# First stage of a graph network: range pairs, edge counts and tile loads in another order, and a buffer of its own for tile 9

## The reference

```
x1  = layernorm(x)
xl  = x1 @ W1;  res = x1 @ Wr1                        # layer 1: 4 heads of 256, "dense" and "res1"
e   = leaky_relu(alpha_src[src] + alpha_dst[dst])      # alpha = sums of xl * a_src1, xl * a_dst1
h   = relu(layernorm(segment_softmax(e) weighted sum of xl[src] + b1)) + res + br1
h   = the same with one head of 768 (W2, Wr2)          # layer 2
x   = x + h
g   = softmax(layernorm(x) @ Fr + fbr);  top 2 of 8 experts per node
out = x + sum over the two experts of g * (gelu(layernorm(x) @ F1[e] + fb1[e]) @ F2[e] + fb2[e])
```

## Time and profile before

| | us |
|---|---|
| median of 3 runs | 1108.69 |
| the runs | 1107.84, 1112.44, 1108.69 |
| the profiled execution, its own time | 1107.56 |
| its span in the trace | 1105.8 |

### The profile page before, as it was taken

The page is one execution under the profiler, slowest core; times in us unless marked ns, Lnnn a source line. Parts: engine busy times, 40 slices in busy tenths (PEclk is TensorE's granted clock), DMA queues, the critical chain, the costliest instruction groups (busy, mean ns, idle before and its releaser), DMA issues.

```text
span 1105.8 us, 15213 instructions
## 1 busy us (share of the span) xinstructions
PE 1048.9 (95%) x4364; PEld 696.6 (63%) x4365; DVE 700.1 (63%) x1708; ACT 357.4 (32%) x632; POOL 140.1 (13%) x266
## 2 busy tenths in 40 slices
PE   5999999999999999999999999999999779999993
PEld 3467777755588888855556556556666546665661
DVE  5998899579677777879466517866777533223222
ACT  0222321233477777611001014820001223333331
POOL 3000010000000000011000000102222213324332
PEclk9999999999999999999999999999999899999997
DMA  9535556611134001072121100332448755484432
GB/s 265 190 115 208 206 202 215 225 44 52 44 117 184 21 1 38 1 200 80 58 75 48 46 29 29 93 147 86 118 117 311 243 196 183 146 306 126 152 108 91
DMA packets 53567, 141.44 MB, mean 128 GB/s; under 512 B 8346, under 2 KB 17082, under 8 KB 53250
## 3 DMA queue, kind: packets, MB, share of 16 engines
q1 hardware_dynamic: 42321, 109.17, 29.4%
q0 software_dynamic: 8160, 23.16, 6.6%
q10 hardware_dynamic: 3024, 8.36, 2.7%
HBM read 81.89 MB, written 61.48 MB: 130 GB/s over the span
## 4 chain that ended last, share of the span: by engine, by line
issue 38%; PE 36%; DMA 11%; DVE 10%; DVEq 2%; POOL 1%; SPq 1%; POOLq 0%; ACT 0%
PE PSA L1887 9%; PE PSA L1828 8%; PE PSA L1817 7%; DMA RX<-out,RX 6%; PE PSA L1947 3%; PE PSA L1961 3%; DVE RW2X L880 2%; DMA out<-RX 2%; DVE RB L894 1%; DVE RX L1244 1%; DVE RW2X L882 1%; DVEq L803 1%; PE PSA L1908 1%; DMA xs_d<-RB,RW2X 1%; DMA RB<-xr_d 1%
## 5 line engine op out<-in xcount | busy, mean ns | idle before, releaser
L1801 PE MATMUL PSA<-RW2X 125*125 125x257 f32 x800 | 173.9, 380 | 0.0
L1801 PEld LDWEIGHTS PSA<-RW2X 125*125 125x125 f32 x800 | 149.8, 188 | 24.4 <-DVE RW2X L962 0.8
L1887 PE MATMUL PSA<-RW2X,RW 125*125 125x385 f32 (+1 forms) x360 | 122.0, 489 | 0.0
L1620 PE MATMUL PSA<-RW,RX 128*125 128x512 f32 x240 | 109.9, 607 | 1.9 <-ACT RX L1319 1.9
L1828 PE MATMUL PSA<-RW2X,RX 128*125 128x384 f32 x320 | 107.3, 488 | 1.9 <-DVE RW2X L1040 1.9
L1638 PE MATMUL PSA<-RW,RX 128*125 128x512 f32 (+2 forms) x360 | 107.4, 452 | 0.0
L1817 PE MATMUL PSA<-RW2X,RX 128*125 128x384 f32 x320 | 105.1, 487 | 2.2 <-ACT RX L1439 1.4
L1428 ACT ACTIVATE RW2X<-RX,RK 125x625 f32<-125x625 f32 x120 | 91.5, 811 | 31.3 <-PE PSA L1801 31.3
L1961 PE MATMUL PSA<-RW2X 128*128 x276 | 96.4, 500 | 2.7 <-issue 1.0
L956 DVE TENSOR_TENSOR RW2X<-RW2X 125x625 f32<-125x625 f32 x80 | 64.8, 810 | 53.7 <-ACT RW2X L1428 53.6
L1947 PE MATMUL PSA<-RW2X,RX 128*128 x276 | 96.4, 499 | 1.9 <-ACT RX L1522 1.1
(11 more groups left out here) (337 smaller groups left out, 1273.0 us busy)
## 6 DMA issues: line engine op xcount, KB each, us to landing
xs_d<-RB SPq DMA_DIRECT2D x10, 3108.0 KB, 11.2
RW2X<-in_L_ffn_W SPq DMA_DIRECT2D x16, 1152.0 KB, 8.3
RW2X<-xs_d ACTq DMA_DIRECT2D x21, 388.5 KB
RX<-res_d SPq DMA_DIRECT2D x10, 448.0 KB
RX<-in_x SPq DMA_DIRECT2D x12, 336.0 KB
RX<-adm_d SPq DMA_DIRECT2D x6, 610.4 KB
xr_d<-RW2X SPq DMA_DIRECT2D x10, 336.0 KB
res_d<-RB SPq DMA_DIRECT2D x7, 448.0 KB
```

What stands on the lines that cost most here:

```text
L1620: last = mm(ps[res_bank(n)][0:TP, :], xTt[t][:, kk, :], wr1s[:, kk, j * 512:(j + 1) * 512], start=(kk == 0), stop=(kk == KD - 1))
L1801: last = mm(ps[n % 7][0:TP, 0:XW], ering[:, (p * NT + m) % EBUF, 0, i * TP:(i + 1) * TP], xl[:, m, p // 2, :], start=(m == 0), stop=(m == ...
L1887: last = mm(ps[PAIR[t % 3][c]][0:TP, 0:DW - c], p2[m][:, t * TP:(t + 1) * TP], xl2[:, m, c, 0:DW - c], start=(m == 0), stop=(m == NT - 1))
```

## The change

In the first stage:

- DVE: the normalisation of tile 0 comes ahead of the conversion of the edge lists; the norm of tile 1 ahead of the wait for PE's edge transposes, instead of behind the table; the 48 sums behind pair 2 and the norm of tile 4, instead of ahead of them.
- PE: half of res1(0) comes ahead of the edge transposes, turn_x(1) and 4 of 6 products of res1(1) ahead of the rows of the ranges. Between the dense products the hists move: hist(2) behind dense(0, 0) and dense(0, 1), dense(1, 0) ahead of dense(0, 2), and turn_x goes from tile t + 4 to t + 3. Tile 0 has one hist fewer, tile 9 two more (`WIN`).
- ACT: its copies follow PE's order; `nth` gives the place of a dense part in the new order.
- SP: the first half of `Wr1` is loaded in two parts with semaphores of their own, and tiles 2 and 3 have their own load ahead of tiles 4 to 9.

In the last layer, tile 9 has a third buffer `xr[2]`, at the start of RX where `ya` (the sum of an expert's output) lies later. Its load stands behind the store of tile 1 and waits for no other store; and `drain(0)`, the first to write `ya`, waits for the store of tile 9.

```diff
-WIN = (2, 2, 2, 2, 2, 2, 3, 3, 3, 2)
+WIN = (1, 2, 2, 2, 2, 2, 2, 3, 3, 4)
...
         ya = f(D)
+        xr.append(ya[0:TP, :])
...
+        def xb(t):
+            return 2 if t == NT - 1 else t % 2
...
-            for j in range(2):
-                sp.dma_start(wr1s[:, :, j * 512:(j + 1) * 512],
...
+            sp.dma_start(wr1s[:, 0:KD // 2, 0:512], wr1_in[:, 0:KD // 2, 0:512]).then_inc(ld_wr1_top, 16)
+            sp.dma_start(wr1s[:, KD // 2:KD, 0:512], wr1_in[:, KD // 2:KD, 0:512]).then_inc(ld_wr1[0], 16)
+            rows(sp, xall[:, 1, :], x_t[1], ld_x1)
+            sp.dma_start(wr1s[:, :, 512:C1], wr1_in[:, :, 512:C1]).then_inc(ld_wr1[1], 16)
+            rows(sp, xall[:, 2:4, :], x_t[2:4].rearrange("t p d -> p t d"), ld_x23)
+            rows(sp, xall[:, 4:NT, :], x_t[4:NT].rearrange("t p d -> p t d"), ld_x)
...
-                rows(sp, out_t[t], xr[t % 2], x1_stored[t % 2])
-                if t + 2 < NT:
+                rows(sp, out_t[t], xr[xb(t)], x1_stored[xb(t)])
+                if t == 1:
+                    load_xr(NT - 1)
+                if t + 2 < NT - 1:
...
             norm_stats(0)
+            norm_apply(0)
             dve.wait_ge(ld_e, 32)
...
-            norm_apply(0)
...
+            dve.wait_ge(ld_x1, 32)
+            norm_stats(1)
 
             dve.wait_ge(edges_turned, 1)
...
             v.tensor_copy(tab_i, tab_f[:, 3, :]).then_inc(table_ready, 1)
-            dve.wait_ge(ld_x1, 32)
-            norm_stats(1)
...
-                if p == 1:
+                if p == 2:
                     wa1_sums()
...
-                if not (isinstance(n, int) and n == 0):
+                if isinstance(n, int) and n == 0:
+                    dve.wait_ge(x1_stored[2], 32)
+                else:
                     dve.wait_ge(y_ready, n)
...
             turn_x(0)
+            pe.wait_ge(xt_ready, 2)
+            pe.wait_ge(ld_wr1_top, 16)
+            res1(0, 0, KD // 2)
             pe.wait_ge(edges_ready, 1)
...
-            pe.wait_ge(xt_ready, 2)
-            res1(0)
+            pe.wait_ge(ld_wr1[0], 16)
+            res1(0, KD // 2, KD)
+            turn_x(1)
+            res1(1, 0, 4)
             pe.wait_ge(range_cols, 1)
...
-            res1(1)
+            res1(1, 4, KD)
...
-                res1(2 * t + 1)
-                turn_x(t + 1)
-            w = 2
-            for t in range(NT):
+                if t == 1:
+                    res1(2 * t + 1, 0, KD // 2)
+                    turn_x(t + 1)
+                    res1(2 * t + 1, KD // 2, KD)
+                else:
+                    turn_x(t + 1)
+                    res1(2 * t + 1)
+            dense(0, 0)
+            dense(0, 1)
+            hist(2)
+            dense(1, 0)
+            dense(0, 2)
+            turn_x(4)
+            hist(3)
+            dense(1, 1)
+            dense(1, 2)
+            hist(4)
+            w = 5
+            for t in range(2, NT):
                 pe.wait_ge(xt_ready, 2 * t + 2)
                 dense(t, 0)
+                if t + 3 < NT:
+                    turn_x(t + 3)
                 hist(w)
                 dense(t, 1)
+                if t >= 7:
+                    hist(w + 1)
                 dense(t, 2)
-                if t + 4 < NT:
-                    turn_x(t + 4)
-                for i in range(1, WIN[t]):
+                for i in range(2 if t >= 7 else 1, WIN[t]):
                     hist(w + i)
```

More of the change, by code:

```diff
@@ L333, in gnn_ffn @@
         ld_x1 = sem("ld_x1")
+        ld_x23 = sem("ld_x23")
         ld_x = sem("ld_x")
@@ L421, in gnn_ffn @@
         norm2_done = sem("norm2_done")
-        xr_loaded = [sem(f"xr_loaded{i}") for i in range(2)]
+        xr_loaded = [sem(f"xr_loaded{i}") for i in range(3)]
         x1_ready = sem("x1_ready")
-        x1_stored = [sem(f"x1_stored{i}") for i in range(2)]
+        x1_stored = [sem(f"x1_stored{i}") for i in range(3)]
         xf_ready = sem("xf_ready")
@@ L461, in gnn_ffn, with nth @@
         block = ctx.enter_context(nc.Block())
+        def nth(t, c):
+            return {(1, 0): 2, (0, 2): 3}.get((t, c), 3 * t + c)
         def res_bank(n):
@@ L489, in _ @@
             sp.dma_start(e_i[:, 1, :], dst.rearrange("(g e) -> g e", g=EG)).then_inc(ld_e, 16)
[L490 to L495 removed]
+            wr1_in = Wr1.rearrange("(k p) c -> p k c", p=128)
+            sp.dma_start(wr1s[:, 0:KD // 2, 0:512], wr1_in[:, 0:KD // 2, 0:512]).then_inc(ld_wr1_top, 16)
[4 more added lines that the diff above has]
+            rows(sp, xall[:, 4:NT, :], x_t[4:NT].rearrange("t p d -> p t d"), ld_x)
             sp.dma_start(abc[:, 0, :], a_src1.rearrange("h c -> (h c)")[None, :].to_broadcast([128, C1])).then_inc(ld_a, 16)
@@ L586, in load_xr @@
             def load_xr(t):
-                rows(sp, xr[t % 2], xr_d[t], xr_loaded[t % 2])
+                rows(sp, xr[xb(t)], xr_d[t], xr_loaded[xb(t)])
             for i in range(2):
@@ L642, in _ @@
                 sp.sem_inc(w_ready, 1)
-            for i in range(2):
-                sp.wait_ge(x1_stored[i], 32 * HT)
+            for i in range(3):
+                sp.wait_ge(x1_stored[i], 32 * (HT, HT - 1, 1)[i])
         @block.gpsimd
@@ L770, in _ @@
             pool.wait_ge(slots_ready, 1)
-            for i in range(2):
-                pool.wait_ge(x1_stored[i], 32 * HT)
+            for i in range(3):
+                pool.wait_ge(x1_stored[i], 32 * (HT, HT - 1, 1)[i])
             total = pool.value_load(slot_i[0:1, 2, 7:8], min_val=EARLY + 1, max_val=30)
@@ L1360, in _ @@
             xt_keep(0)
-            for t in range(R0 // 2):
+            norm(1)
+            xt_keep(1)
+            res_keep(0)
+            res_keep(1)
+            for t in range(1, R0 // 2):
                 res_keep(2 * t)
                 norm(t + 1)
-                if t:
-                    hist_keep(t - 1)
+                hist_keep(t - 1)
+                xt_keep(t + 1)
                 res_keep(2 * t + 1)
-                xt_keep(t + 1)
-            w = 2
-            for t in range(NT):
+            dense_keep(0, 0)
+            dense_keep(0, 1)
+            hist_keep(2)
+            norm(4)
+            dense_keep(1, 0)
+            dense_keep(0, 2)
+            xt_keep(4)
+            hist_keep(3)
+            dense_keep(1, 1)
+            dense_keep(1, 2)
+            hist_keep(4)
+            w = 5
+            for t in range(2, NT):
+                if t + 3 < NT:
+                    norm(t + 3)
                 dense_keep(t, 0)
-                if t + 4 < NT:
-                    norm(t + 4)
+                if t + 3 < NT:
+                    xt_keep(t + 3)
                 hist_keep(w)
                 dense_keep(t, 1)
+                if t >= 7:
+                    hist_keep(w + 1)
                 dense_keep(t, 2)
-                if t + 4 < NT:
-                    xt_keep(t + 4)
-                for i in range(1, WIN[t]):
+                for i in range(2 if t >= 7 else 1, WIN[t]):
                     hist_keep(w + i)
@@ L1682, in _ @@
             mm(ps[2][0:1, 64:64 + NW], lhc[:, 2:3], ident[0:NW, 0:NW], start=True, stop=True).then_inc(range_rows, 1)
-            res1(1)
+            res1(1, 4, KD)
             pe.wait_ge(consts, 1)
             pe.wait_ge(table_ready, 1)
-            turn_x(1)
             for t in range(1, R0 // 2):
```

27 lines of the change are left out of this document (12 added, 15 removed).

## The result

The changed kernel takes 1102.56 us (median of 15 runs), the kernel before 1105.83 in 15 runs beside it; the ratio is 0.9957, 95% interval 0.9939 to 0.9976, so about 4.7 us less. One of the 15 runs took 2847.79 us and is left out of the ratio. The forecast was 10.2 us less and 1098.5 us. Its base was the first median of 3 runs, 1108.69, which the later runs put 2.9 us lower; the time lies 4.1 us above the forecast and inside its range. Faster was right, and a little less than half of the forecast gain came.

A forecast was written before the change was run, and what follows sets the result against it. PE was taken to bound the first stage, with DVE close behind and bounding it after the change. Stage -3.3, tile 9 -4.1 and its clock -2.8 sum to -10.2 us: 1098.5 us, range 1095.0 to 1104.5.

The forecast's parts named there:

- The start: First stage: DVE's first window at T + 10.3 = 29.5 us against 30.14, its block moved by -0.6 us.
- T: First stage: time at which PE has finished the edges, put between 17.7 and 20.3 us, taken as 19.2.
- the distance between the two moves only as a block: First stage: DVE runs freely from first window (30.14 us) to last window's end (209.31), so that span only shifts.
- DVE's 21 pauses average 0.5 us: First stage: DVE's issue pauses, put down to instruction fetch; a few more or fewer move either end by 1 us.
- PE stops being the bound, and DVE becomes it: First stage's end: PE's last hist would end at 207.8 us, DVE's last window later, at 208.7.
- rival 3: First stage: PE remains the bound and takes all its idle back; -5.4 us there, 1096.4 us; chance within the forecast's 0.62.
- The end: First stage's end: two hists behind dense(9, 2) let PE transpose at 210.05 instead of 213.39; stage 3.3 us earlier.
- Rival 2: First stage: DVE's windows start no earlier and the stage gains nothing; 1101.8 us; chance 0.12 (a third with rival 1).
- The sums a pair later: First stage: DVE's moved sums end at 68.9 us, ahead of dense(0, 2) at 70.8, covered by 1.9 us.
- Tile 9: Last layer: own buffer ends DVE's 4.22 us wait, PE gets it 4.1 us earlier; full clock gives 2.8 us more.
- rival 1: Last layer: the clock stays low at tile 9, leaving -7.4 us in all, 1101.3 us; chance 0.14.
- Rival 4: Last layer: tile 9's store holds the first drain and the loop; slower from a landing about 897 us; chance 0.03.

The follow-up runs named there:

- experiment 4: Kernel before with the ten zeroing writes to xs_d moved behind the first stage: ratio 1.0035 (1.0007 to 1.0064) to the kernel before.
- experiment 6: Changed kernel with six zeroing writes each behind a late res1 store and four at 325 us: 1096.01 us, ratio 0.9924 to the kernel before.
- experiment 8: Kernel of experiment 6 with dense(9, 2) put behind the last two hists, the order of before: ratio 0.9944 to the kernel before.
- experiment 2: Kernel before with only tile 9's own buffer added: ratio 0.9951 (0.9927 to 0.9975) to the kernel before.
- experiment 3: Changed kernel with the ten zeroing writes to xs_d moved behind the first stage: ratio 0.9934 (0.9908 to 0.9961) to the kernel before.
- experiment 5: Changed kernel with both range words of a pair loaded ahead of its first window: ratio 1.0017 (1.0000 to 1.0034) to the kernel before.
- experiment 9: Kernel of experiment 6 plus ten thin writes (1024 rows, 0.4 MB each) at the old places in the stage: ratio 0.9911 to the kernel before.
- experiment 10: Kernel of experiment 6 plus ten wide writes (128 rows, 3.1 MB each) at the old places in the stage: ratio 0.9937 to the kernel before.
- experiment 11: Kernel of experiment 2 with the zeroing writes spread as in experiment 6: ratio 0.9977 (0.9960 to 0.9994) to the kernel before.
- experiment 1: Changed kernel with tile 9 back in the shared row buffers, so the stage's change alone: ratio 0.9998 (0.9978 to 1.0019) to the kernel before.

## Why the prediction was right, and where it was wrong

- **The start: right.** T was bounded by 17.7 and 20.3; it was 17.6, the fast end: the edges, from 15.45 on, took 2.2 us, near the 2.1 of the fast pace. "First window: T + 10.3" gives 27.9; it was 28.12.
- **The failed step** is in the first part: "the distance between the two moves only as a block", and then "DVE's 21 pauses average 0.5 us [...] a few more or fewer of them move either end by 1." The block grew by 3.7 us and the pauses by 5.0. With the writes away 5.3 us of pauses are left in the kernel before and 5.4 in the changed one (experiments 4 and 6):

```profile
DVE RW2X L879 <- issue: 5.3, 12, 1.3
```

```profile
DVE RW2X L893 <- issue: 5.4, 11, 1.6
```

  So half of the 10.6 us and two thirds of the 15.6 were register loads beside writes, and not the loading of code, by which the prediction explained them with the Trainium skill, "Runtime: NRT & Kernel Launch", section Instruction fetch mechanics; what the other 5.3 are is open. (The split is rough: with the writes away DVE also waits 4.6 and 4.3 us for PE, and a pause that falls into such a wait doesn't show.) Where the writes fall is set by PE's dense parts: the first starts 3.8 us earlier than before, the others about 8, and 25 slow loads beside ten writes stand against 17 beside nine. The views read gave a sum of pauses; the loads' own row, 300/308/954, already showed two kinds. With T = 17.6 and the old block the last window would have ended at 207.3, the low end of the forecast; eight more slow loads at 0.5 us each are 4, about the 3.7 us of difference.
- **"PE stops being the bound, and DVE becomes it": right as a reading of this kernel, wrong as a law.** It is DVE that ends the stage here, but only because of the slow loads. PE's own end was put at 207.8 for T = 19.2, so 206.2 for 17.6; where PE did bound (experiment 6) its last hist ended at 206.85. That is rival 3, which needed DVE to "stall less than before", and it took moving the writes to get it.
- **The end: the mechanism right** (experiment 8, 1.8 us). From the last window to the transposes it took 1.85 us and not 1.35: PE's waits of 1.5 and 1.9 us stand in front of a stretch at a granted clock of 0.57, in which the last 8 products of hist took 2.00 us where the 8 before took 1.11. Rival 2's outcome came (a stage that gains nothing, 1101.8 us), but not by its mechanism, since the windows did start early. So for the stage it was luck that the time fell inside the range: it is wide enough to hold a stage that gains nothing.
- **The sums a pair later: right**, no wait of PE for them.
- **Tile 9: right.** -4.1 was -3.7 (x1 of tile 9 at 861.06, with the layer 0.6 us late); the clock stayed up, and the two together brought 7.0 us by that scatter, net of the 0.6, for 6.9 forecast. PE idled 2.0 us and not 0.9. By the ratio of experiment 2 it is 5.4 us, 2.8 to 8.1. What lies between may be rival 1: in experiment 3 PE waited 2.1 us at the same place, the clock fell, and the scatter came at 889.45:

```profile
863.00:868.00 5.00, 3.11 (x12) 2.51 (x12) 2.76 (x17) 1.92 (x7) 0.58 (x2) 0.68 1.02 410
868.00:873.00 5.00, 5.00 (x18) 4.09 (x19) 2.96 (x21) 0.38 (x2) 1.62 (x2) 0.50 0.81 330
```

  It is common: of the nine profiles with tile 9's buffer and no doubled writes, five (experiments 3, 5, 6, 8 and 9) have a granted clock under 1.00 somewhere from 858 to 878 us (in 6, 8 and 9 already from about 860 on, ahead of tile 9), and four (the changed kernel, 2, 10 and 11) have 1.00 throughout. Of the other runs only the mean clock is on record; in 14 of the changed kernel it is 0.982 to 0.989, mostly the lower the longer the run. Where it fell in them is not known, so how much of the difference is rival 1 stays open.
- **Rival 4: no.** SP's load of the third expert came at 858.11 ("about 856" was forecast), the store of tile 9 was issued at 862.11, and the first drain at 883.19 waited for ACT and not for the store.

By terms: stage -3.3 forecast, about 0 measured (experiment 1); tile 9 and its clock -6.9 forecast, -5.4 (-2.8 to -8.1) measured (experiment 2). The range's ends by their own terms are 1094.8 and 1104.6, not 1095.0 and 1104.5, which changes nothing here.

## What to carry to other kernels

- Where an engine's list is bound by loops whose bounds it reads from memory, look at the register loads' own row (shortest, median, longest) and lay the long loads beside the DMAs. A sum of "issue" pauses hides this.
- Moving one engine's pieces also moves every DMA that they set off. Ask which other engine's register loads the new moment falls on; large writes with slack belong into a stretch where nobody reads registers in a loop, but ahead of no load that is soon needed.
- A change at one chain can be worth nothing until a second one is out of its way: the same stage was worth nothing with the writes beside it and 5.9 us without.

## What the runs showed of the hardware that I had not expected

- DVE's load of one word from the core's own memory into a register took 0.30 us, and about 0.9 to 1.0 us in the first 7 us of a 3.1 MB write to DRAM; a load that started 7.6 us or more behind the write's start took 0.30 to 0.34, though the write's packets ran on to 9 to 11 us. Beside reads at about 400 GB/s DVE's took 0.30 to 0.44 and SP's 0.27. Why a write slows it, and why its end does not, is open.
- The Trainium skill, "Runtime: NRT & Kernel Launch", section Instruction fetch mechanics, gives about 200 ns a register for the runtime's register loads from HBM and calls loads round trips. The 0.30 here, for a load of another kind, is of that size, and no run tells whether a round trip is what the writes stretch.
- PE's granted clock fell to 0.57 after three waits of 0.8, 1.5 and 1.9 us with about 1.1 us of products between them, and did not fall at tile 9 after one of 2.0, where in experiment 3 it did after 2.1.
